# A three-stage audio tower rebuilt on TensorE: 512-token tiles, features ordered by expert, a mixer in logarithms and 32-row score tiles

## The reference, cut to what matters

```python
# x: (8, 256, 128), float32
zf, zi, zh = x @ Wf + bf, x @ Wi + bi, x @ Wh + bh
diff = softplus(-zf) - softplus(-zi)
log_f, log_i = -softplus(diff), -softplus(-diff)
log_val = concat([log(0.5), log_i + log_g(zh)])     # log_g(z) = log(relu(z)+0.5) if z>=0 else -softplus(-z)
a_star = concat([0, log_f])
h = exp(a_star + cumlogsumexp(log_val - a_star))    # (8, 257, 128); position 0 is 0.5

n = layernorm(h)                                    # no weights
q, k, v = n @ q_w.T, n @ kv_w.T                     # 8 heads of 16; k, v of batch b come from batch b +- 4
h = h + softmax(q k^T / sqrt(128)) v

xf = layernorm(h)
z = swiglu5(xf @ shared_w1 + shared_b1, shared_act) @ shared_w2 + shared_b2   # width 96
w = top-2 of softmax(xf @ gate_w + gate_b), normalised                        # 16 experts
oe = swiglu5(xf @ expert_w1 + expert_b1, expert_act) @ expert_w2 + expert_b2  # all 16, width 96
h = h + z + sum_e w_e oe_e
# swiglu5: g, u = clipped even and odd columns; g * sigmoid(g*alpha) * scale * (u + shift)
```

## Time and profile before

| what | value |
|---|---|
| median of 3 runs | 390.45 us (390.0 to 390.88) |
| profiled execution, span | 388.2 us |
| the profiled execution's own time beside that span | not listed; the runs' median lies 2.2 us over the span |
| PE busy, matmuls | 316.8 us, 82% |
| DVE busy | 298.8 us, 77% |
| ACT busy | 243.1 us, 63% |
| POOL busy | 158.3 us, 41% |
| read from and written to memory | 11.63 MB and 5.28 MB |

### The profile page before, as it was taken

The page is one execution under the profiler, slowest core; times in us unless marked ns, Lnnn a source line. Parts: engine busy times, 40 slices in busy tenths (PEclk is TensorE's granted clock), DMA queues, the critical chain, the costliest instruction groups (busy, mean ns, idle before and its releaser), DMA issues. The chain is left out here.

```text
span 388.2 us, 6049 instructions
## 1 busy us (share of the span) xinstructions
PE 316.8 (82%) x2160; PEld 258.7 (67%) x2160; DVE 298.8 (77%) x500; ACT 243.1 (63%) x412; POOL 158.3 (41%) x125
## 2 busy tenths in 40 slices
PE   3427028986968999999899999979999998879873
PEld 1105027854667878788588787968787887768752
DVE  7894646722579969978998999887976788887990
ACT  2684521542684858597598685675773877485751
POOL 1000372101032874744348577342234445357752
PEclk9767755798986999999999999989999999999998
DMA  7500850000390000008400000075000000000000
GB/s 270 221 0 0 220 80 2 0 3 0 117 183 0 2 3 1 0 3 218 56 28 2 2 3 0 2 207 67 28 2 0 3 2 0 0 31 3 0 1 27
DMA packets 12414, 17.30 MB, mean 45 GB/s; under 512 B 984, under 2 KB 9184, under 8 KB 12256
## 3 DMA queue, kind: packets, MB, share of 16 engines
q1 hardware_dynamic: 12384, 16.91, 17.6%
HBM read 11.63 MB, written 5.28 MB: 44 GB/s over the span
## 5 line engine op out<-in xcount | busy, mean ns | idle before, releaser
L506 POOL TENSOR_TENSOR te<-tbuf,ubuf 128x516 f32<-128x516 f32 x52 | 73.8, 1424 | 50.4 <-DVE tbuf L882 27.6
L956 PE MATMUL slot<-xh,w1h 128*128 128x258 f32 x208 | 64.7, 311 | 13.0 <-DVE xl L865 4.0
L495 POOL TENSOR_TENSOR ubuf<-ubuf,cwb 128x516 f32<-128x516 f32 x24 | 34.3, 1429 | 67.2 <-ACT cwb L659 48.9
L956 PE MATMUL slot<-xh,w1l 128*128 128x258 f32 x208 | 59.9, 288 | 0.0
L956 PE MATMUL slot<-xl,w1h 128*128 128x258 f32 x208 | 59.8, 288 | 0.0
L956 PE MATMUL slot<-te,w 128*128 128x258 f32 x208 | 50.7, 393 | 4.2 <-POOL te L506 3.5
L956 PEld LDWEIGHTS slot<-xh,w1h 128*128 128x128 f32 x208 | 40.3, 194 | 19.4 <-issue 14.0
L882 DVE SCALAR_TENSOR_TENSOR tbuf<-tbuf,gbuf 128x516 f32<-128x516 f32 x52 | 48.3, 935 | 6.0 <-ACT tbuf L666 5.6
L781 DVE TENSOR_REDUCE mx<-slot 128x2 f32<-128x514 f32 x64 | 41.6, 687 | 12.6 <-PE slot L956 12.4
L956 PEld LDWEIGHTS slot<-te,w 128*128 128x128 f32 x208 | 39.6, 195 | 12.8 <-POOL te L506 6.4
L646 ACT ACTIVATE gbuf<-slot,cst 128x516 f32<-128x516 f32 x52 | 35.8, 690 | 19.2 <-PE slot L956 16.8
(11 more groups left out here) (161 smaller groups left out, 614.6 us busy)
## 6 DMA issues: line engine op xcount, KB each, us to landing
qs<-spill SPq DMA_DIRECT2D x12, 258.0 KB, 4.5
ks<-spill SPq DMA_DIRECT2D x24, 129.0 KB, 5.9
spill<-qhl SPq DMA_DIRECT2D x4, 516.0 KB, 2.8
spill<-khl SPq DMA_DIRECT2D x4, 516.0 KB, 3.4
pt<-in_w SPq DMA_DIRECT2D x1, 1664.0 KB, 9.5
xt<-in_x SPq DMA_DIRECT2D x4, 256.0 KB, 5.4
out<-osb SPq DMA_DIRECT2D x8, 128.0 KB
te<-in_sel SPq DMA_DIRECT2D x1, 832.0 KB, 11.0
```

The costliest lines, as they stand in the source:

```text
L495: g.tensor_tensor(ubuf[:, c % NB, :, :], ubuf[:, c % NB, :, :], cwb[:, :, :], ALU.mult).then_inc(S["ucw"], 1)
L506: g.tensor_tensor(te[:, c % NTE, :, :], tbuf[:, c % NB, :, :], ubuf[:, c % NB, :, :], ALU.mult)\
L956: return nc.tensor.matmul(out_, lhsT, rhs, start=start, stop=stop, **k)
```

## The change

The kernel is written anew. The reference and the four units stay; what differs:

- **Tiles of 512 tokens.** W = 2 * T = 512: two sides of 256 tokens in one PSUM bank, with no padding. The position ahead of them is the same for all tokens before attention, and its normalised value is zero, so its query, key and value are zero: in attention it adds exp(-max) to each sum (`e0`, `o0`, and `mz` clips the maxima at 0). Its output row is computed once for all eight batches at the end (pieces with names in z).
- **Features by expert.** The 16 experts have 1,536 features in `ROUTED` = 12 chunks; row p of each chunk belongs to expert p // 8, so one tile of weights `cwb` serves all twelve. The shared expert is chunk 13, without weights. Biases sit in row 0 of w1, where the normalised tokens are overwritten by ones (`one`). A half is one f32 matmul of 512 columns. w1 arrives in two arrays that are subtracted on GpSimd (`w1p`, `w1s`), which takes the row-0 part out of every row.
- **Evictions and products.** Chunks go in pairs of 1,024 columns (`NP` = 7 pairs k, the last of one chunk). VectorE evicts the gate half with its clip; ScalarE copies the up half and GpSimd clips six of seven pairs (`UP_BY`); VectorE weights four pairs and GpSimd two (`CW_BY`); the last products are shared (`TE_BY`). Residual and biases are summed with the down products in one PSUM bank (`y0`).
- **Mixer in logarithms.** ScalarE makes log(1+exp(-|z|)) for all three projections; TensorE adds and subtracts the logarithms in PSUM through (negative, halved) identities (`lsum`, `wsum`, `wm`, `fsum`); VectorE scans a running maximum and the state. One table set serves it and the attention.
- **Scores on 32 rows.** q and k stay in SBUF. The queries or keys of one of two heads are masked (`qm`, `km`), and a score matmul takes the 32 rows of one pair of heads: four row groups, four banks. A second 32-row matmul (`onesr`, `nm`) subtracts the maxima. Nothing is spilled to memory.
- **PSUM** is eight banks (`BANKS`), placed by a table (`BANK_OF`). New order tables for all engines.

```diff
-W = N + 1
+W = 2 * T
...
+UP_BY = ("AG", "AG", "AG", "AG", "AG", "AG", "V")
+CW_BY = ("V", "V", "V", "G", "V", "G", "")
+TE_BY = ("G", "V", "G", "V", "G", "V", "V")
...
 AT = {
     "P": (
+        2, 0, 1, 6, 7, 8, 9, 11, 13, 18, 17, 22, 23, 24, 26, 27, 29, 34, 41, 35, 52, 42, 46, 55, 30, 31, 37, 38, 45,
...
+BANK_OF = (
+    0, 1, 2, 3, 4, 5, 6, 7, 0, 2, 1, 5, 3, 6, 4, 7, 1, 0, 2, 5, 3, 6, 4, 1, 5, 7, 2, 3, 6, 4, 5, 7, 2, 3, 5, 7, 4,
...
-                for s in range(2):
-                    o = slot(st, name)[:, s, 0:W]
-                    mm(o, w1h[:, k, c, :], xh[:, s, :], stop=False)
-                    mm(o, w1h[:, k, c, :], xl[:, s, :], start=False, stop=False)
-                    last = mm(o, w1l[:, k, c, :], xh[:, s, :], start=False)
-                fill(last, st, name)
...
+            def half_(u, c, name, kind):
+                ge(pe, "one", u + 1)
+                pe.wait_ge(s_w1, W1_SET)
+                ps.take(pe, name, u, c)
+                ps.fill(mm(ps.bank(name, u, c)[:, :], w1_of(c, kind), xn2[:, u % 2, :]), name, u, c)
...
+            def lsum(u):
...
+                mm(o, wd[:, :], xt[:, u, :], stop=False)
...
+                mm(o, hident, z3[:, 0, :], start=False, stop=False)
+                mm(o, nhident, z3[:, 1, :], start=False, stop=False)
+                ge(pe, "l3", u + 1)
+                mm(o, ident, l3[:, 0, :], start=False, stop=False)
+                ps.fill(mm(o, nident, l3[:, 1, :], start=False, stop=True), "lsum", u)
...
+            def st(u, s, c, h):
+                ge(pe, "qm", 2 * u + 2)
+                ps.released(pe, "k", u)
+                for t in (2 * h, 2 * h + 1):
+                    ps.take(pe, "st", u, s, c, t)
+                for t in (2 * h, 2 * h + 1):
+                    rows = slice(32 * t, 32 * t + 32)
+                    mm(ps.bank("st", u, s, c, t)[:, :], kt[rows, 1 - s, c * P:(c + 1) * P],
+                       qm[rows, s, :, :].rearrange("p i t -> p (i t)"), stop=False)
+                ge(pe, "nm", 2 * u + s + 1)
+                for t in (2 * h, 2 * h + 1):
+                    rows = slice(32 * t, 32 * t + 32)
+                    ps.fill(mm(ps.bank("st", u, s, c, t)[:, :], const("onesr")[rows, :],
+                               nm[rows, s, :, :].rearrange("p i t -> p (i t)"), start=False, stop=True), "st", u, s, c, t)
...
+            def up_clip(u, k):
+                n = NP * u + k
+                ps.released(pool, "u", u, chunks(k)[-1])
+                v_ = halves(k, vr, n % NV)
+                r = col(2 * k)
+                g.tensor_scalar(v_, v_, fpar[:, UHI, r:r + 1], fpar[:, ULO, r:r + 1], ALU.min, ALU.max).then_inc(S["ucg"], 1)
```

1757 lines of the change are left out of this document (939 added, 818 removed), and 114 rows, old and new, of tables (AT, BANK_OF, BY, ENGINES).

## The result

The changed kernel takes **400.43 us** (median of 4 runs, 399.92 to 402.51) beside 390.66 us for the kernel before on the same chip: a ratio of **1.026**, 95% interval 1.023 to 1.029. On a second chip the pair gave 400.78 and 393.71 us, 1.020 (1.014 to 1.026). The forecast was 378 us and faster. The sign is wrong; the time lies inside the range of 358 to 408.

A forecast was written before the change was run, and what follows sets the result against it. The prediction took TensorE (PE) as the bound: opening to 113 us, 243 us of PE work at 94.7% as 257 to 370, 5 us of tail, 2.2 outside the span, giving 378 us. Four fifths of the probability lay in 358 to 408.

The forecast's parts named there:

- What bounds the kernel before: Kernel before, 120 to 360 us: PE, 94.7% busy, sets the pace; DVE at 86% is next.
- Prices by start distances: PE matmuls priced by distance between starts: 0.857 us per f32 matmul of 512 columns, 0.121 per fp32r one of 258.
- The opening: Start of the run: first score tile at 49 us, first expert half at 113 us, with 92 us of PE work placed before.
- The score term: Attention's maxima and scores on PE: 54.7 us, from 48 groups of four row tiles at 0.91 and some 17 lone pieces.
- only in twos: Slower rival for the attention's row tiles: they overlap only in pairs, 82 us instead of 55, total 407 us; chance 0.12.
- The rest at 94.7%: After the first expert half: 243 us of PE work at 94.7% busy take 257 us, to 370.
- a clock of 0.5 after 120 us: Sign, after the opening: the forecast is wrong if PE's granted clock returns to 0.5.
- Cover: Expert products: PE's surplus of about 100 us over DVE was to hide work moved between GpSimd and VectorE.
- The title's two moves: Expert evictions: six clips on GpSimd and four weightings on VectorE, claimed to be worth nothing in themselves.
- The mis-sized terms of the other engines: Engine totals off PE's path: DVE 205 to 245 us, ACT near 225, POOL near 120; none bounds a stretch for long.
- PE full less often: Slower rival: PE waits on eight single banks; at 88% full the rest takes 276 us, total 397 us; chance 0.17.
- the five cases: Whole-run outcomes: 366 to 394 us (chance 0.55), 360 (0.12), 397 (0.17), 407 (0.12), 494 (0.04).

The follow-up runs named there:

- a_again: The changed kernel run once more, unaltered, on the chip of three other runs: 400.78 us, 1.020 of the kernel before.
- a_tail: Changed kernel with GpSimd's last weighting and last product of the last unit moved to VectorE: 396.28 us, 1.008 of the kernel before.

## Why the prediction was wrong, point by point

**What bounds the kernel before: half right.** PE sets its pace against more work (+12 us of PE, +11 us of time). But I read 94.7% for PE and 86% for VectorE as one bound and one also-ran. They are two bounds: less work on PE brings nearly nothing.

**Prices by start distances: right for full matmuls.** Halves that follow each other without a wait start 0.858 to 0.860 us apart, the forecast was 0.857; down products 1.72 a pair. That one f32 half costs more than the fp32r triples was said in the prediction, and the run with f32 halves in the kernel before puts a time on it, 11 us.

**The opening: right.** First score tile at 51.17 us (49 forecast), first expert half at 116.11 (113), and this although the granted clock was 1.00 all through the opening, where I had put the first matmuls at the slow clock.

**The score term, first failed step.** I had 54.7 us for maxima and scores; they take 71.3 (23.8 and 47.5). There are 21 maxima groups and 42 score groups in the order, 63, and 65 in my count, so the number was right. Their price was not: 1.07 us for a maxima group, 0.96 for one of a score piece, where I had 0.91; and the 17 lone pairs, for which I had 11 us in all, 0.65 each, cost the same as four tiles. 21 x 1.07 + 42 x 0.96 = 62.8, 8 us more than I had. The other 8.5 us are no price: 4.0 are idle time of PE, 3.2 of it for ScalarE's exponentials, and the score pieces from 261.75 us take 6.1 us instead of 3.8, more than half of that time at the lower clock. Four row tiles in 1.07 us are 3.2 times as fast as four times 0.857, in 0.96 us 3.6 times. The figure of the Trainium skill (TensorE: Matmul & The Clock Gate, Measured speedup vs the span model), 3.07 times, gave 1.12 us: the trace of the maxima groups agrees with it, and I had set it aside for the column tiles of the earlier trace rows, which overlap completely and are no model for row tiles. The rival "only in twos" fails as worded: four do overlap; and its price of 82 us is farther from 62.8 than mine.

**The rest at 94.7%, second failed step.** PE was busy for 95.4% of 120 to 360 us, which looks like the forecast. But this share counts PE at half the clock as busy, and it leaves out the end. From the first expert half to the end of the last down product are 273.9 us. My sum allowed 13.6 us there for all that is not work. The trace has 16.3 us of idle time and 20.5 us at the lower clock, which cost another 9.8: 26.1 us. What is left, 247.8 us, is 90.5% and not 94.7%. The prediction had named a clock of 0.5 after 120 us as a sign that it is wrong, and it came four times. With both other engines shortened the stretch from 120 to 360 is 97.2% full, and the two losses are 7.6 and 4.9 us, 12.5 in all: my allowance would have fitted a kernel without the product chain.

**Cover, the third failed step, and what stands behind the second.** "The title's two moves are worth nothing in themselves; their cover is PE's surplus of about 100 us over DVE." PE's surplus was even larger, 139 us (364.4 less 225.1), and it did not cover the moves in this order: four clips a unit back on VectorE cost 8 us, six cost 43, both moves turned around 62. The surplus is a sum over the run. Within a unit the steps between a half's eviction and its down product are a chain over three engines, with three tiles of `yr` and `vr` and four of `tr` between them, and each engine takes its queue in order. In the changed kernel this chain adds 13 us of span, for which my sum had no term of its own. It is most visible in the last unit, where nothing else is left to do: a wait of 3.44 us, and 3.1 us more (seven passes in 6.1 us instead of 3.0) for the clock it lost.

**The mis-sized terms of the other engines** did no harm. A clip on GpSimd measures 1.53 us (1.2 forecast, 1.19 without VectorE beside it); an eviction on VectorE 0.80 us (0.69); VectorE in all 225 (205 to 245 forecast), GpSimd 122 (120), ScalarE 195 (225).

**The sum.** The forecast span was 375.5 us, the measured one is 398.2, 22.7 more. Three are the opening. Some 12 are the idle time and the lower clock behind it (26.1 us less the 13.6 allowed). Some 8 are more work behind it: 247.8 us at the full clock, where I had 243 less the 3.4 at the very end. Of these 11 us in the opening and in the work, 8 are the price of the row tile groups; where the other 3 lie stays open. Neither failed step alone turns the sign. With the groups at their measured price the forecast would have been 378 + 8.1 / 0.947 = 386.6 us, still faster; with the waits and the clock as measured, 390.5, the time of the kernel before; with both, 399.

The rival "PE full less often" (397 us, deciding from 91%) is the one that came nearest, with 90.5%. Its reason, banks that come free late, is half of it: behind 120 us PE waits some 8 us for evictions and exponentials and 5.3 us for the products of GpSimd and VectorE. It did not name the clock.

**The chances.** The range of the five cases held the time, but 0.62 for faster rested on one unmeasured price, for which a row of another shape was taken over a page's figure for the very shape, and on a busy share carried over from another kernel. That 397 lies so near the measured 400.4 is in part luck: two errors of some 8 and 12 us, of which that rival had one.

## What to carry to other kernels

Price every matmul form by the distance between starts, for its own tile shape: a row tile is not a column tile, and a pair of row tiles costs what four cost. An engine's busy share does not say whether a step can be moved onto it; in the run with all clips on VectorE what decided was what stood ahead of the step in that engine's queue and who waited behind it, so ask for each moved step which instruction comes before it and when that can start. Read the clock beside the busy share: here PE was busy for 94% of the time between the first half and the last down product, and 90.5% is what it was worth at the full clock. Where two engines were both over 85% busy, as in the middle of the kernel before, 12 us more work on one cost 11 us, and 50 us less brought 7.

## What the runs showed of the hardware that I had not expected

- Two row tiles of 32 rows by 512 f32 columns take as long as four: 1.06 and 1.07 us to the next work. The f32 passes of such a group are 0.53 us apart, those of a full matmul 0.43.
- VectorE and GpSimd lengthen each other's SBUF operations, on average: VectorE's weighting 1.23 to 1.80 us, its gate product 1.22 to 1.52, GpSimd's clip 1.19 to 1.53, its product 2.35 to 2.82. VectorE's evictions and maxima, which read PSUM, are untouched.
- A wait of 3.44 us of PE was followed by seven passes at the lower clock (0.85 us apart, 1.2 GHz), nearly as costly again as the wait; in the profile of `a_again`, the same kernel, three passes followed the same wait at that clock. Behind one of 1.08 us (`a_tail`) the passes stayed at 0.43, but the clock also fell behind two waits of 0.71 and 0.95 us and, without any wait, 4.6 us into a row of 52 instructions of 8 columns. In the run with VectorE's operations shortened this last one (318.3 to 325.1 us, the narrow instructions start from 314.2 to 321.2) is the only low stretch before the last down product.
- VectorE clips 1,024 columns in 0.81 us when GpSimd's weightings are short and in 0.92 to 1.32 on average when they are not, less than the 1.53 of GpSimd, and with this order the kernel is still faster with GpSimd doing it.
